# A selective scan in VMamba style on one core: C multiplied in step by step, softplus in a PSUM bank, y summed in three parts, dt*u on VectorE

## The reference

```python
dts, Bs, Cs = jnp.split(x_dbl, [R, R + N], axis=2)        # R = 24, N = 16
dts = jnp.einsum('bkrl,kdr->bkdl', dts, dt_projs_w)
dts = jax.nn.softplus(dts + dt_projs_b[None, :, :, None])
As = -jnp.exp(A_logs).reshape(K, DI, N)                   # DI = 192, K = 4 directions
...
dA = jnp.exp(d_t[..., None] * As)
h = h * dA + (d_t * u_t)[..., None] * B_t[:, :, None, :]
y = jnp.einsum('bkcn,bkn->bkc', h, C_t)
...
return ys + Dsk[None, :, :, None] * xs
```

## Time and profile before

| What | us |
|---|---|
| median of 3 runs | 1902.5 (1901.48 to 1925.6) |
| the profiled execution, its own time | 1899.44 |
| its span, first to last instruction | 1897.6 |
| of this busy: PE | 1593.9 (84%) |
| DVE | 1296.1 (68%) |
| POOL | 1097.6 (58%) |
| ACT | 1003.4 (53%) |
| mean granted clock of TensorE | 0.872 of full |

### The profile page before, as it was taken

The page is one execution under the profiler, slowest core; times in us unless marked ns, Lnnn a source line. Parts: engine busy times, 40 slices in busy tenths (PEclk is TensorE's granted clock), DMA queues, the critical chain, the costliest instruction groups (busy, mean ns, idle before and its releaser), DMA issues. The chain is left out here.

```text
span 1897.6 us, 65044 instructions
## 1 busy us (share of the span) xinstructions
PE 1593.9 (84%) x30152; PEld 1075.7 (57%) x30152; DVE 1296.1 (68%) x938; ACT 1003.4 (53%) x1860; POOL 1097.6 (58%) x222
## 2 busy tenths in 40 slices
PE   7897579797987979797798978788897766998998
PEld 5654456565655656565565656556565532665565
DVE  5872286878687777868777786887778887354211
ACT  2233666666565667667566666756566520212112
POOL 0111178687786968778786977778696964020000
PEclk8896588988898988899898989989898987688989
DMA  9234013132122222221221312122221243010101
GB/s 310 89 126 164 13 43 82 53 83 68 52 61 63 78 64 79 61 64 51 74 79 52 89 48 76 47 79 70 64 75 50 70 155 151 0 59 9 67 21 46
DMA packets 47583, 141.56 MB, mean 75 GB/s; under 512 B 7990, under 2 KB 16694, under 8 KB 46800
## 3 DMA queue, kind: packets, MB, share of 16 engines
q1 hardware_dynamic: 47312, 137.39, 23.9%
HBM read 104.86 MB, written 32.51 MB: 72 GB/s over the span
## 5 line engine op out<-in xcount | busy, mean ns | idle before, releaser
L851 DVE TENSOR_TENSOR_SCAN s_h<-s_a,s_pb 128x1024 f32<-128x1024 f32 x384 | 866.6, 2278 | 316.9 <-PE s_pb L687 279.8
L883 POOL TENSOR_TENSOR s_h<-s_h,s_crow 128x3072 f32<-128x3072 f32 x128 | 883.7, 6916 | 316.0 <-DVE s_h L851 316.0
L687 PE MATMUL s_pb<-k_area,s_dtut 64*64 64x64 f32 x24576 | 496.5, 237 | 131.1 <-DVE s_h L851 114.1
L687 PEld LDWEIGHTS s_pb<-k_area,s_dtut 64*64 64x64 f32 x24576 | 447.1, 149 | 222.1 <-DVE s_h L851 142.2
L776 ACT ACTIVATE s_a<-s_dup,s_aneg 128x1024 f32<-128x1024 f32 x384 | 437.4, 1144 | 44.5 <-DVE s_h L851 43.9
L702 PE MATMUL s_py<-s_h,k_mask 128*64 128x512 f32 x1024 | 271.7, 651 | 7.4 <-POOL s_h L883 5.0
L764 ACT ACTIVATE k_area<-k_mask,s_bt 128x64 f32<-128x64 f32 x1024 | 265.5, 340 | 0.0
L743 ACT COPY s_dup<-s_pm 128x512 f32<-128x512 f32 x96 | 106.3, 1108 | 200.4 <-PE s_pm L669 200.3
L669 PE MATMUL s_pm<-k_eye,y_y 128*64 128x128 f32 x1536 | 123.8, 312 | 88.7 <-DVE y_y L834 76.4
L669 PEld LDWEIGHTS s_pm<-k_eye,y_y 128*64 128x64 f32 x1536 | 99.8, 157 | 119.8 <-issue 97.8
L589 POOL TENSOR_TENSOR k_area<-s_bt,k_mask 128x2048 f32<-128x2048 f32 x32 | 116.3, 3633 | 34.7 <-ACT s_bt L743 34.7
(11 more groups left out here) (156 smaller groups left out, 1533.6 us busy)
## 6 DMA issues: line engine op xcount, KB each, us to landing
s_crow<-scratch_xd SPq DMA_DIRECT2D x256, 256.0 KB, 4.0
k_area<-in_x_dram SPq DMA_DIRECT2D x4, 1536.0 KB, 7.9
scratch_xt<-h_xt SPq DMA_DIRECT2D x4, 1536.0 KB, 10.1
k_u<-scratch_u SPq DMA_DIRECT2D x12, 512.0 KB, 5.0
y_y<-scratch_y SPq DMA_DIRECT2D x4, 1536.0 KB, 11.0
k_area<-scratch_xt SPq DMA_DIRECT2D x4, 1536.0 KB, 8.6
out_dram<-t_out SPq DMA_DIRECT2D x32, 192.0 KB, 1.9
scratch_xd<-h_dbl SPq DMA_DIRECT2D x8, 512.0 KB, 2.6
```

The costliest lines, as they stand in the source:

```text
L687: mm = pe.matmul(pb[par * HALF:(par + 1) * HALF, step % 2, r * BANK + blk:(r + 1) * BANK:BLK], dtut[here, u % 2, blk, g * HALF:(g + 1) * H ...
L851: nc.vector.tensor_tensor_scan(h[:, step % (TRIPLES * CG), f], a[:, step % RING, f], pb[:, step % 2, f], 0.0, ALU.mult, ALU.add).then_inc( ...
L883: nc.gpsimd.tensor_tensor(h[:, at:at + CG], h[:, at:at + CG], crow[:, n % CROWS].unsqueeze(1).broadcast_to([P, CG, L]), ALU.mult).then_inc ...
```

## The change

It has six parts.

1. **C step by step.** POOL multiplies after every scan, 128x1024, instead of 128x3072 after every third.
2. **y in three parts.** `add_y` is cut in three: two calls (four instructions) behind each `spread_b`, `LAG` = 7. A slot of `h` is free when its own part is done.
3. **Softplus in `pm`.** Behind ACT's ln, which now writes to the PSUM bank, DVE's four instructions are done on 512 columns at a time, in three rounds: 12 instructions, each with one operand in SBUF and one in PSUM, two behind each scan of steps 9 to 14. ACT's ln is three instructions.
4. **dt in column order.** A `DUP` chunk is now 16 calls with 64x64 tiles that write every eighth column, so that ACT's copy out of the bank is contiguous. `BT` uses `pe.transpose`.
5. **dt*u on DVE**, one 128x1536 instruction at step 15, both inputs in SBUF.
6. **Other slots.** `Z` at steps 0 to 3, `BT` at 4, `UT` at 5 to 8, `DUP` at 17 to 22; ACT's rows of B over more steps.

```diff
-LAG = 8
+LAG = 7
+ROUNDS = 3
...
-    return {"Z": 2, "BT": 6, "UT": 7, "DUP": 14}[what] + i
+    return {"Z": 0, "BT": 4, "UT": 5, "DUP": 17}[what] + i
...
-                        mm = pe.matmul(pm[:, blk * N:(blk + 1) * N], tokens(rows[PR:PR + N], blk), eye[PR:PR + N, PR:PR + N],
-                                       start=True, stop=True)
+                        mm = pe.transpose(pm[:, blk * N:(blk + 1) * N], tokens(rows[PR:PR + N], blk), eye[PR:PR + N, PR:PR + N])
...
-                    g, hq = i // 2, i % 2
-                    for x in range(4):
+                    pe.wait_ge(dt_ready, ROUNDS * (u + 1))
+                    g, r = i // 2, i % 2
+                    here = slice(r * HALF, (r + 1) * HALF)
+                    for blk in range(BLK):
                         for par in range(2):
-                            mm = pe.matmul(pm[par * HALF:(par + 1) * HALF, x * P:(x + 1) * P],
-                                           zs[:, 4 * hq + x, g * HALF:(g + 1) * HALF], eye[:], start=True, stop=True)
+                            mm = pe.matmul(pm[par * HALF:(par + 1) * HALF, blk::BLK], dt_of[here, blk, g * HALF:(g + 1) * HALF],
+                                           eye[here, here], start=True, stop=True)
...
-            def add_y(n):
+            def add_y(n, part):
...
-                pe.wait_ge(hc_ready, n + 1)
-                if first:
+                if first and part == 0:
                     need(pe, y_taken, 2 * taken(b, o))
                 at = n % TRIPLES * CG
-                for q in halves():
+                if part < 2:
+                    pe.wait_ge(hc_ready, CG * n + 2)
+                    q = halves()[part]
                     for g in range(2):
-                        pe.matmul(py[g * HALF:(g + 1) * HALF, q], mask[:], h[:, at + g, q], start=first, stop=last)
-                for lh, q in enumerate(halves()):
-                    mm = pe.matmul(py2[lh * HALF:(lh + 1) * HALF], mask[:], h[:, at + 2, q], start=first, stop=last)
+                        mm = pe.matmul(py[g * HALF:(g + 1) * HALF, q], mask[:], h[:, at + g, q], start=first, stop=last)
+                else:
+                    pe.wait_ge(hc_ready, CG * n + 3)
+                    for lh, q in enumerate(halves()):
+                        mm = pe.matmul(py2[lh * HALF:(lh + 1) * HALF], mask[:], h[:, at + 2, q], start=first, stop=last)
                 mm.then_inc(y_added, 1)
...
+            def logarithm(u, r):
+                act.wait_ge(exp_ready, u + 1)
+                act.wait_ge(chunk_taken, CHUNK[u, "DUP", 0])
+                need(act, dt_ready, ROUNDS * u + r)
+                nc.scalar.activation(pm[:], ez[:, round_cols(r)], ACT.Ln, bias=1.0).then_inc(ln_ready, 1)
...
-                    nc.vector.scalar_tensor_tensor(wz, wz, -1.0, ez, ALU.add, ALU.subtract).then_inc(lost_ready, 1)
+                    dve.wait_ge(ln_ready, count)
+                    nc.vector.scalar_tensor_tensor(pm[:], wz[:, at], -1.0, pm[:], ALU.add, ALU.subtract).then_inc(short_ready, 1)
...
-                    nc.vector.scalar_tensor_tensor(lz, ez, LN2, lz, ALU.mult, ALU.max).then_inc(log_ready, 1)
+                    nc.vector.scalar_tensor_tensor(pm[:], ez[:, at], LN2, pm[:], ALU.mult, ALU.max).then_inc(floor_ready, 1)
...
+            def times_u(u):
+                dve.wait_ge(dt_ready, ROUNDS * (u + 1))
+                dve.wait_ge(chunk_taken, CHUNK[u - u % 2, "UT", 3] + 1)
+                need(dve, b_row, STEPS * (u - 1))
+                nc.vector.tensor_tensor(dtut[:, u % 2].rearrange("p k c -> p (k c)"), zs, ut[:].rearrange("p k c -> p (k c)"),
+                                        ALU.mult).then_inc(dtu_ready, 1)
...
-                nc.gpsimd.tensor_tensor(h[:, at:at + CG], h[:, at:at + CG],
-                                        crow[:, n % CROWS].unsqueeze(1).broadcast_to([P, CG, L]), ALU.mult).then_inc(hc_ready, 1)
+                nc.gpsimd.tensor_tensor(h[:, at], h[:, at], crow[:, n % CROWS], ALU.mult).then_inc(hc_ready, 1)
```

More of the change, by code:

```diff
@@ L530, in scan @@
         dsum = sb("dsum", [P, 2])
-        wide = [ys[k][:].rearrange("p a l -> p (a l)").rearrange("p (x k c) -> p x k c", x=2, k=BLK) for k in ("y0", "y1")]
-        zs, ez, wz, lz = (wide[i][:, x] for i in range(2) for x in range(2))
+        wide = [ys[k][:].rearrange("p a l -> p (a l)").rearrange("p (x m) -> p x m", x=2) for k in ("y0", "y1")]
+        zs, ez, wz = wide[0][:, 0], wide[0][:, 1], wide[1][:, 0]
+        dt_of = zs.rearrange("p (k c) -> p k c", k=BLK)
         ut = sb("ut", [P, BLK, DI])
@@ L713, in _ @@
                     spread_b(u, i)
-                    if step >= LAG and (step - LAG) % CG == 0:
-                        add_y((step - LAG) // CG)
+                    if step >= LAG:
+                        add_y((step - LAG) // CG, (step - LAG) % CG)
                     if u + 1 < UNITS:
@@ L719, in _ @@
                                 chunk(u + 1, *what)
-            for n in range((LAST - LAG + CG - 1) // CG, LAST // CG):
-                add_y(n)
+            for step in range(LAST - LAG, LAST):
+                add_y(step // CG, step % CG)
         @block.scalar
@@ L790, in _ @@
                 if what[0] == "BT":
-                    for part in range(4):
-                        softplus(0, part)
+                    for part in range(3):
+                        exponent(0, part)
+                if what == ("DUP", 0):
+                    for r in range(ROUNDS):
+                        logarithm(0, r)
                 take_chunk(0, *what)
-            for piece in (0, 2):
-                build_rows(0, piece, 0, 4 * BLK)
+            build_rows(0, 0, 0, 4 * BLK)
+            build_rows(0, 2, 0, 2 * BLK)
             act.wait_ge(aneg_ready, 1)
@@ L857, in _ @@
             dve.wait_ge(dsum_ready, 1)
-            for part in range(4):
-                softplus(0, part)
+            for r in range(ROUNDS):
+                for part in range(4):
+                    softplus(0, r, part)
+            times_u(0)
             for u in range(UNITS):
```

98 lines of the change are left out of this document (50 added, 48 removed).

## The result

Four runs of the changed kernel took 1837.48 us in the median (1830.46 to 1842.58); four of the kernel before, taken with them, 1913.69 (1901.48 to 1925.6). The ratio is 0.96, its 95% interval 0.9508 to 0.9691: faster, and 11 us above the forecast of 1826. The profiled execution took 1842.58 us, its span is 1840.8, and its mean granted clock 0.902, where the one before had 0.872.

What follows compares the result with a forecast made beforehand. Bound: the handover between PE and DVE, with DVE waiting for `spread_b`. Profiled 1899.4 us, less 73 over fifteen units (79.2 each), plus 2.4 before the first scan, less 6 at the end, is 1823; 3 more for the median: 1826, range 1765 to 1888.

Steps and rivals of the forecast that it cites:

- below 75 per unit nothing can go: Floor on a unit's time, from PE busy 66 us of a unit and DVE 64.
- Part 1: Softplus in PSUM escapes the DVE/POOL port block: twelve instructions at 0.75 us, 9.0 per unit with handing over, against 11.4.
- rival of dear writes to PSUM: DVE's softplus instructions take 1.1 us each, adding 4.2 per unit: 1889 us in all, chance 0.11.
- Part 2: dt*u on DVE at step 15: 1.73 us plus 0.8 for its turn against POOL, together 2.5 per unit.
- slower: PE idles 1.6 us per step in steps 9 to 16, its clock falls, 10 us per unit: 1975 us, chance 0.06.
- Part 3: POOL's step-by-step products take 2.37 us each, 64.8 of work per unit; no wait for POOL expected.
- Part 4: A third of `add_y` takes PE 1.01 us, so a bare step is 2.10, just below DVE's 2.20.
- Part 5: PE's chunks: `BT` 2.0 us, up to 3.0; `DUP` 0.95, between 0.55 and 1.1; ACT's shorter copy gains nothing.
- 6 x 3.05 - 0.95: Ledger entry for steps 17 to 22 of a unit: six steps of 3.05 us less 0.95 of saved slack, 17.4.
- Part 6: `take_y` at steps 6 and 7 loses its cover: 1.5 to 1.9 us in half of the units, 0.85 per unit.
- The clock: Of 3.9 us per unit put down to TensorE's lower clock, 1.4 stay, since L831's stall goes and `BT` halves.
- rival of a clock that does not mind: All 3.9 us of clock cost stay, 81.75 per unit: 1864 us in all, chance 0.17.

Runs made afterwards that it cites:

- b2: Changed kernel with the edits of e1, e5 and e7 together: 1748.23 us in the median of 6 runs, ratio to before 0.9164.
- e2: Changed kernel with softplus's twelve instructions on SBUF buffers in place of the PSUM bank, still three rounds: 2029.93 us in one run.
- e1: Changed kernel with dt*u back on POOL: 1781.65 us in the median of 4 runs, ratio to before 0.9256.
- e7: Changed kernel with `DUP` in the old row order, eight calls of 128x64 tiles with 128 moving columns per chunk: 1796.28 us in one run.
- e5: Changed kernel with ACT's half of `take_y` at step 5, ahead of a softplus activation, instead of step 6: 1823.97 us in one run.
- b1: Changed kernel with the edits of e1 and e5 together: 1765.79 us in the median of 6 runs, ratio to before 0.9235.
- e8: Changed kernel with `DUP` as in e7, each call cut in two of 64 columns, so 32 instructions per chunk: 1827.34 us in one run.
- e9: Changed kernel with the loads of u issued three pairs of states later: 1831.39 us in one profiled execution.
- e3: Changed kernel with `BT` by matmul in place of `pe.transpose`, 16 instructions for 8: 1873.95 us in one run.
- e4: Changed kernel with the three parts of `add_y` called together behind every third `spread_b`: 1831.9 us in one run.
- e6: Changed kernel with C multiplied over three steps in one POOL instruction again, y still in three parts: 1851.3 us in one run.
- e10: The kernel of e8 with the loads of u issued three pairs of states later: 1834.61 us in one profiled execution.

## Why the prediction was right, and where it was not

Faster by over 2% was given 0.77, the time lies in the range, and the step that carried it, a unit of 79.2, was measured at 79.49. But that agreement is partly luck: four stretches of the unit were off by more than 1 us, two in each direction. And the floor, "below 75 per unit nothing can go", was wrong: it didn't follow from PE's 66 and DVE's 64, and b2 is at 73.49.

**Part 1, softplus in the bank**: the mechanism holds, e2 shows it from the other side. The price was over: 0.67 to 0.70 per instruction and 1.31 per pair, not 0.75 and 1.5, so steps 9 to 14 are 21.05 for 22.2. The Trainium skill's formula (VectorE: DVE Perf Modes, TRN2 errata), quoted in the prediction as 0.66, is closer than my row L843 was. My lower bound of 0.62 had no ground: it takes 0.1 us to start, where the rows of L842 and L843 leave 0.22. The rival of dear writes to PSUM is out.

**Part 2, dt*u on DVE**: the first of the two failed steps. I took 1.73 and 0.8 for its turn, because at step 15 it "starts directly behind a scan whose end also releases POOL". That assumed POOL idle. The row at 830.64 has POOL at the first of five products back to back, since it builds rows of B at step 13 and is behind; it was 0.9 us into it when dt*u came, and dt*u waits 1.3 for its end: 3.05, the same in all 15 units (45.5 us in 15). e1 gives 4.0 per unit: 3.0 of the step and 1.1 behind it in steps 17 to 22. In the 3 us PE has finished `spread_b`, its part of y and a chunk and idles 2.0 to 2.1 for the scan, and the granted clock falls:

```profile
836.96 1.16 PE L693 MATMUL s_pb<-k_area,s_dtut 64*64 64x64 f32 x64 [2.00 <-DVE s_h L884]
...
839.77 1.57 PEld L675 LDWEIGHTS s_pm<-k_eye,y_y 64*64 64x64 f32 x27 [1.53 <-issue]
```

27 loads in 1.57 us, where 28 take 0.89 further on in the same unit: the lower level, 1.2 GHz. The clock falls there in 12 of the 15 units, and with dt*u on POOL (e1) in none. So the rival named *slower* was right in its mechanism and wrong in its place and size: in steps 9 to 14, where PE idles 1.6 at a time, the clock is full in all 15 units, and it falls behind the idle 2.0 of dt*u. What the fall costs shows in e7, which has hardly a stop: steps 17 to 22 take 17.9 us in ten units where the clock falls, 16.32 in the four where it doesn't. So it is 1.6 us, and not 10; it takes back what PE saves up in the long step 15.

That also says what the 1.1 is. In odd units steps 17 to 22 take 18.13 us in the changed kernel, with the fall in five of seven, and 18.21 in e1, without it. All of the 1.1 is in the even units (20.75 and 18.55), where PE's instructions come late, and half of it in unit 4 alone. The same edit between e5 and b1 gives 3.32, so the loss is 3.0 for the step and 0.3 to 1.1 behind it. I should also have priced the alternative: POOL needed 3.47 for it, and by my own sum had 64.8 us in a unit of 79.

**Part 3, POOL**: 2.43 us in the mean for 2.37, and it is never waited for in units with chunks. The surplus is dt*u again: POOL's product that meets it takes 3.86, in each of 15 units, and the others about 2.37. The sum leaves out that even 2.37 is more than a bare step. In the last unit, at 2.19 a step, POOL falls behind; its last ten products run from 1453.24 to 1476.48, and PE's sum waits:

```profile
1453.24 23.24 POOL L917 TENSOR_TENSOR s_h<-s_h,s_crow 128x1024 f32<-128x1024 f32 x10
1454.03 13.15 DVE L884 TENSOR_TENSOR_SCAN s_h<-s_a,s_pb 128x1024 f32<-128x1024 f32 x6
...
1474.23 0.29 PEld L709 LDWEIGHTS s_py<-s_h,k_mask 128*64 128x64 f32 x4 [4.24 <-POOL s_h L917]
```

**Part 4, y in parts**: a bare step is 2.19, as worked out (2.20), and DVE's 0.74 behind three scans are gone. I had counted it in the units and not in the last one, which gained 6.9; and the 6 I had counted behind the last scan were 1.3. The two errors leave 2.2.

**Part 5, the chunks**: `BT` is 0.95 to 0.98, not 2.0; steps 0 to 4 are 16.19 for 17.3. I scaled the number of instructions and took the time of one from the earlier trace rows, but in transpose mode one is half as long too. `DUP` itself is 1.01 of loads, inside my 0.55 to 1.1. The second failed step is what I made of steps 17 to 22, "6 x 3.05 - 0.95": the steady step is 3.05, but the clock behind dt*u takes the saved slack back, and PE's instructions run out, a cost that the sum had at nothing. Where neither happens, in units 3 and 9, the steps take 16.54 and 16.98; the mean is 19.53. e7 and e8 put a price on the 32 instructions: 17.75 us for 16, 18.83 for 32 in the same order. The Trainium skill (Runtime: NRT & Kernel Launch, Instruction fetch mechanics) says that the sequencer fetches its next instructions by a DMA queue of its own, and calls the cost "mostly hidden". The trace agrees on the queue, and not on the cost here: 13.1 us of stops in 15 units, each ending just behind a packet of this queue, and clock and slack lost behind them. That loads of u make the packets late is shown less firmly: they start later while such loads are in flight (2.0 us for 0.7), and e9 takes the surplus of the even units away, but stops also occur without them, as in unit 14.

**Part 6, take_y**: 1.5 to 1.9 in half of the units was right in size for DVE's half (step 6 is 4.01 for 2.2), though that is DVE's own two instructions and not a wait for `spread_b`, which comes on top at step 7 with 0.2 to 1.7. ACT's half is another matter: DVE waits 5.81 where I had 1.5 to 1.9, in three units, so 0.8 us more per unit. I had looked at the two DVE instructions only, and not at what stands ahead of ACT's copy in its queue.

**The clock**: of 3.9 us per unit I kept 1.4. Time at the lower level fell from 272 to 110 us in 15 units, so from 18 to 7 us each; at half speed that is 9 against 3.7 of PE's work, much of it hidden. The direction was right, and the rival of a clock that does not mind (1864) is out. Both causes that I named hold up: e3 brings the fall behind `BT` back in every unit, and none is left in steps 9 to 15, where the stall of L831 was. What I had at nothing is the new fall behind dt*u. In 14 of 15 units the `spread_b` behind the `BT` transposes runs at full clock (64 loads in 1.02). The Trainium skill (TensorE: Matmul & The Clock Gate, PE-mode transpose) says that a transpose doesn't count as TensorE's work for the clock in the way a matmul does; a chunk of 1 us, with other work on both sides, shows nothing of such a loss, and no run here has a longer one.

**The sum.** Units: 15 x 4.58 = 68.7 us gained for 73. Ahead of the first scan +2.5 for +2.4. Last unit and its end -8.2 for -6. That is -74.4 for -76.6. The miss in the profiled execution (1842.58 for 1823) is in the tail, whose code the change doesn't touch: 357.3 us, before 339.7. Its first two windows of 50 us, in the kernel before and in the changed one:

```profile
1557.87:1607.87 50.00, 32.04 (x97) 16.36 (x97) 41.26 (x90) 8.96 (x21) 19.79 (x19) 0.73 0.51 194
1607.87:1657.87 50.00, 49.58 (x164) 30.04 (x164) 18.69 (x55) 13.34 (x26) 0.00 (x0) 0.64 0.00 0
```

```profile
1483.49:1533.49 50.00, 31.66 (x68) 13.94 (x68) 37.55 (x81) 8.67 (x21) 19.78 (x19) 0.53 0.50 194
1533.49:1583.49 50.00, 50.00 (x134) 26.71 (x134) 16.45 (x39) 7.28 (x20) 0.00 (x0) 0.53 0.00 1
```

The same work at granted clock 0.53. Of 14 profiled executions, eight (before, e3, e4, e6, e7, e10, b1, b2) have a tail of 336 to 340 us; e8 and e9 have 351 and 352, and the changed kernel, e1, e2 and e5 have 357. e8 and e10 differ in one move of a load, far ahead of the tail. The scatter of the runs has the same size (1901 and 1925 before, 1764 and 1783 in e1). The four of 357 us are at the lower clock level in one stretch from 7 to 89 us behind the tail's start, where the others have two of some 20 us; e8 and e9 start like those others (0.74 in the first 50 us) and have an added one of 34 us further on. What sets it stays open. The code of the tail is the same, so I count it as no part of the change's worth; whether the changed kernel comes to the long tail more often than the one before, one profiled execution of each can't tell.
